# Two attentions of a one-core layer chain: another order of the steps, other PSUM banks, and turns by identity products

## The reference, cut to what matters

```python
def global_latent_attn(x, ...):            # local: k, v straight from x, and a window of 32
    q = split_heads(x @ wq, 16)
    latent = x @ w_kv_down                 # 32 wide
    k, v = split_heads(latent @ w_k_up, 4), split_heads(latent @ w_v_up, 4)
    q, k = qk_norm(rope(q)), qk_norm(rope(k))
    return merge_heads(sdpa(q, repeat_kv(k), repeat_kv(v), causal)) @ wo
x = x + global_latent_attn(rmsnorm(x, norm1_w), ...)
x = x + local_gqa_attn(rmsnorm(x, norm2_w), ...)
```

```python
xn = layernorm(x) * ln_g + ln_b
q, k, v = (xn @ W + b for each of q, k, v)      # 16 heads of width 8
w = softmax(q . k * scale, over the keys)
y = (w . v).reshape(B, T, 128)
```

## Time and profile before

| what | before |
|---|---|
| median of three runs | 2624.93 us (2624.47 to 2628.53) |
| the profiled execution, and its span | 2637.31 us, 2635.2 us |
| mean granted TensorE clock, share of full speed | 0.843 |
| PE busy | 2160.3 us (82%), 13860 matmuls |
| PE weight loads busy | 1691.5 us (64%) |
| DVE busy | 1468.8 us (56%) |
| ACT busy | 1000.2 us (38%) |

### The profile page before, as it was taken

How to read it: one execution, slowest core, us unless ns; L and a number is a source line. 1 busy time by engine, 2 the same in 40 slices (tenths; PEclk the granted TensorE clock), 3 DMA queues, 4 the chain that set the end, 5 groups by cost and what they waited for, 6 DMA issues and landing times. The chain is left out here.

```text
span 2635.2 us, 40558 instructions
## 1 busy us (share of the span) xinstructions
PE 2160.3 (82%) x13860; PEld 1691.5 (64%) x13860; DVE 1468.8 (56%) x3930; ACT 1000.2 (38%) x2247; POOL 131.4 (5%) x191
## 2 busy tenths in 40 slices
PE   3588777766997788499899989999979997588875
PEld 2344444435996322399899967888879995355543
DVE  6633334365666899756632226777742227655547
ACT  2244333333222332122244435555534444333434
POOL 2100000020000100100000000000000000000000
PEclk9776756677998899599989989999979998666678
DMA  5000000000000000000000004444300000000000
GB/s 155 2 1 0 0 1 0 0 28 1 1 0 1 0 0 0 32 1 0 1 1 0 0 19 132 125 125 124 123 12 0 0 0 0 1 1 0 0 1 16
DMA packets 47119, 59.65 MB, mean 23 GB/s; under 512 B 7089, under 2 KB 44689, under 8 KB 46323
## 3 DMA queue, kind: packets, MB, share of 16 engines
q1 hardware_dynamic: 47023, 58.43, 7.3%
HBM read 32.20 MB, written 26.21 MB: 22 GB/s over the span
## 5 line engine op out<-in xcount | busy, mean ns | idle before, releaser
L701 ACT ACTIVATE m2a_hid<-psum,m_b 128x256 f32<-128x256 f32 x256 | 100.2, 474 | 114.6 <-PE psum L55 114.5
L701 ACT ACTIVATE m2b_hid<-psum,m_b 128x256 f32<-128x256 f32 x256 | 100.2, 474 | 114.6 <-PE psum L55 114.5
L686 PE MATMUL psum<-m_w,m2a_hid 128*128 128x128 f32 x1024 | 126.2, 277 | 0.0
L686 PE MATMUL psum<-m_w,m2b_hid 128*128 128x128 f32 x1024 | 126.2, 277 | 0.0
L686 PEld LDWEIGHTS psum<-m_w,m2b_hid 128*128 128x128 f32 x1024 | 122.1, 194 | 0.6
L686 PEld LDWEIGHTS psum<-m_w,m2a_hid 128*128 128x128 f32 x1024 | 122.1, 194 | 0.6
L719 DVE SCALAR_TENSOR_TENSOR m2b_acc<-psum,m2b_gates,m2b_acc 128x128 f32<-128x128 f32 x128 | 39.0, 347 | 148.7 <-PE psum L686 148.7
L719 DVE SCALAR_TENSOR_TENSOR m2a_acc<-psum,m2a_gates,m2a_acc 128x128 f32<-128x128 f32 x128 | 39.0, 347 | 148.3 <-PE psum L686 148.3
L2026 ACT ACTIVATE a_p<-a_p,a_nmax 128x256 f32<-128x256 f32 x128 | 64.0, 500 | 143.3 <-DVE a_nmax L2053 143.3
L1769 DVE TENSOR_REDUCE a_nmax<-psum 128x2 f32<-128x512 f32 x128 | 83.0, 687 | 50.3 <-PE psum L1610 50.3
L1056 DVE TENSOR_TENSOR_SCAN a1s_clamped<-a1s_clamp_coef,a1s_bounds 128x1024 f32<-128x1024 f32 x48 | 108.6, 2265 | 0.0
(11 more groups left out here) (608 smaller groups left out, 5728.7 us busy)
## 6 DMA issues: line engine op xcount, KB each, us to landing
a_scratch<-a_pos SPq DMA_DIRECT2D x64, 384.0 KB, 2.7
a_shifted<-a_scratch SPq DMA_DIRECT2D x64, 256.0 KB, 3.1
m_w<-in_m_w SPq DMA_DIRECT2D x1, 2048.0 KB
arena<-in_m_w SPq DMA_DIRECT2D x1, 2048.0 KB, 9.2
arena<-in_m_up SPq DMA_DIRECT2D x1, 1760.0 KB, 7.1
a_w<-in_a_w SPq DMA_DIRECT2D x1, 1536.0 KB, 7.8
out<-X SPq DMA_DIRECT2D x1, 1024.0 KB, 5.1
m_down<-in_m_down SPq DMA_DIRECT2D x1, 880.0 KB
```

The source lines that it names most:

```text
L686: last = nc.tensor.matmul(ps_y(e % 2)[:, t * D:(t + 1) * D], hid[:, e % 2, c * SEQ + t * P:c * SEQ + (t + 1) * P], m.m2_w2[:, e, c, :], st ...
L701: last = nc.scalar.activation(hid[:, e % 2, c * SEQ:(c + 1) * SEQ], ps_up(e % 2)[:, c * SEQ:(c + 1) * SEQ], ACT.Gelu, bias=m.m2_b1[:, e * ...
```

## The change

In both functions the list of steps at each g is another, and some steps write to other banks.

- Grouped attention, PE: turn_back, `end_a`, `end_b` and `start_a` to `start_d` stand at other groups; `ps_y` lies in bank 4 instead of 7; start_d waits for normalise (n, 0) and for end_c of the unit before the present one (y_used). The ten transposes of start_d become ten products with `ident_r`, a float32r copy of the identity, the stack being the stationary operand as before.
- Grouped attention, DVE, ACT and GpSimd: steps regrouped accordingly; the input's norm is computed two units ahead instead of one, for which `threaded_two_ahead` unrolls six copies of the unit instead of four.
- a3: turn_back goes to bank 7 (j = 0, 1) or 5 (j = 2, 3), one group later, as does ACT's move_values; `values` waits for move_values (av_moved) instead of normalise; start_b stands behind values; turn_stack, turn_shifted and turn_back have new waits for their banks; the 24 transposes of a unit become products with `ident_r`.

The diff; its last pieces, from ps_back as a function on, are of a3.

```diff
+def threaded_two_ahead(eng, first, unit, tail):
+
+    first()
+    unit(0, 0, False, True, True)
+    with eng.Fori(0, NB // 2 - 2) as i:
+        unit(1, 2 * i + 1, True, True, True)
+        unit(0, 2 * i + 2, True, True, True)
+    unit(1, NB - 3, True, True, True)
+    unit(0, NB - 2, True, True, False)
+    unit(1, NB - 1, True, False, False)
+    tail(1, NB - 1)
...
-        ps_y = m.psum[:, 7, SEQ:2 * SEQ]
+        ps_y = m.psum[:, 4, 0:SEQ]
...
             def start_d(u, n):
                 pe.wait_ge(qk_ready, n + 1)
                 if not isinstance(n, int) or n:
-                    pe.wait_ge(o_ready, 4 * n - 2)
+                    pe.wait_ge(o_ready, 4 * n - 3)
+                if not isinstance(n, int) or n > 1:
+                    pe.wait_ge(y_used, n - 1)
                 for t in range(PAIR):
                     for j in range(4):
-                        nc.tensor.transpose(m.psum[:, 4 + j // 2, (j % 2) * SEQ + t * P:(j % 2) * SEQ + (t + 1) * P],
-                                            qs[:, t, KV * j:KV * (j + 1), :].rearrange("p h f -> p (h f)").bitcast(F32), m.ident[:, :])
-                    last = nc.tensor.transpose(ps_back[:, t * P:(t + 1) * P], ks[:, t, :, :].rearrange("p h f -> p (h f)").bitcast(F32), m.ident[:, :])
+                        nc.tensor.matmul(m.psum[:, 4 + j // 2, (j % 2) * SEQ + t * P:(j % 2) * SEQ + (t + 1) * P],
+                                         qs[:, t, KV * j:KV * (j + 1), :].rearrange("p h f -> p (h f)"), ident_r[:, :], start=True, stop=True)
+                    last = nc.tensor.matmul(ps_back[:, t * P:(t + 1) * P], ks[:, t, :, :].rearrange("p h f -> p (h f)"), ident_r[:, :], start=True, stop=True)
                 last.then_inc(qkT_ready, 1)
 
...
 
             def turn_back(u, n, j):
                 pe.wait_ge(av_moved, 4 * n + j + 1)
-                if j:
+                if j or not isinstance(n, int) or n:
                     pe.wait_ge(o_ready, 4 * n + j)
-                elif not isinstance(n, int) or n:
-                    pe.wait_ge(y_used, n)
+                if j == 1 and (not isinstance(n, int) or n < NB - 1):
+                    pe.wait_ge(kT_ready, n + 2)
                 for t in range(PAIR):
                     last = nc.tensor.transpose(ps_back[:, t * P:(t + 1) * P], ov[:, j % 2, t * P:(t + 1) * P], m.ident[:, :])
                 last.then_inc(back_ready, 1)
...
-                    if next and g == 6:
-                        start_d(1 - u, n + 1)
+                    if g == 0 and prev:
+                        turn_back(1 - u, n - 1, 2)
+                        values(1 - u, n - 1, 3)
+                    if g == 2 and prev:
+                        turn_back(1 - u, n - 1, 3)
+                    if g in (4, 6):
+                        turn_back(u, n, g // 2 - 2)
                     if g in (2, 4, 6):
                         values(u, n, g // 2 - 1)
-                    if g == 0 and prev:
-                        values(1 - u, n - 1, 3)
-                    if next and g == GROUPS - 1:
+                    if g < 3 and next:
+                        (start_a, start_b, start_c)[g](1 - u, n + 1)
+                    if g == 3 and prev:
+                        end_a(1 - u, n - 1)
+                    if g == 4 and prev:
+                        end_b(1 - u, n - 1)
+                    if g == 5 and next:
+                        start_d(1 - u, n + 1)
+                    if g == 7 and next:
                         pe.wait_ge(e_ready, GROUPS * n + g)
                         ready(n + 1)
                         scores(1 - u, n + 1, 0)
-                    if g in (4, 5, 7):
-                        turn_back(u, n, {4: 0, 5: 1, 7: 2}[g])
-                    if prev and g == 1:
-                        turn_back(1 - u, n - 1, 3)
-                    if prev and g == 2:
-                        end_a(1 - u, n - 1)
-                    if prev and g == 3:
-                        end_b(1 - u, n - 1)
-                    if next and g in (1, 2, 3):
-                        {1: start_a, 2: start_b, 3: start_c}[g](1 - u, n + 1)
...
+                start_a(1, 1)
+                start_b(1, 1)
                 start_e(0, 0)
...
-                    if next and g == 1:
-                        start_b(1 - u, n + 1)
-                    if prev and g == 1:
-                        normalise(1 - u, n - 1, 3)
-                    if next and g == 0:
-                        start_a(1 - u, n + 1)
-                    if prev and g == 3:
-                        end_c(1 - u, n - 1)
-                    if prev and g == 5 and local:
-                        residual_end(nc, dve, m, xn, n - 1)
-                    if next and g == 4:
+                    if g in (0, 2) and prev:
+                        normalise(1 - u, n - 1, 2 + g // 2)
+                    if g == 3 and next:
                         start_d(1 - u, n + 1)
+                    if g == 4 and next:
+                        start_d2(1 - u, n + 1)
                     if g == 4:
                         normalise(u, n, 0)
-                    if next and g == 5:
-                        start_d2(1 - u, n + 1)
-                    if g == 5:
+                    if g == 5 and prev:
+                        end_c(1 - u, n - 1)
+                    if g == 5 and next:
+                        start_e(1 - u, n + 1)
+                    if g == 6 and prev and local:
+                        residual_end(nc, dve, m, xn, n - 1)
+                    if g == 6 and later:
+                        start_a(u, n + 2)
+                    if g == 6:
                         normalise(u, n, 1)
-                    if next and g == 7:
-                        start_e(1 - u, n + 1)
-                    if g == 7:
-                        normalise(u, n, 2)
+                    if g == 7 and later:
+                        start_b(u, n + 2)
...
-        ps_av, ps_back = m.psum[:, 6, 0:SEQ], m.psum[:, 6, SEQ:2 * SEQ]
+        ps_av = m.psum[:, 6, 0:SEQ]
+        ps_back = lambda j: m.psum[:, 7 if j < 2 else 5, 0:SEQ]
...
-                        last = nc.tensor.transpose(out[:, j, t * P:(t + 1) * P], st[:, t, a, heads, :].rearrange("p h f -> p (h f)").bitcast(F32),
-                                                   m.ident[:, :])
+                        last = nc.tensor.matmul(out[:, j, t * P:(t + 1) * P], st[:, t, a, heads, :].rearrange("p h f -> p (h f)"), ident_r[:, :],
+                                                start=True, stop=True)
...
+                    if r == 1 and (not isinstance(n, int) or n > 1):
+                        pe.wait_ge(o_ready, 4 * n - 4)
...
             def turn_shifted(u, n, half):
                 pe.wait_ge(shift_ready, 2 * n + half + 1)
+                if half == 0 and (not isinstance(n, int) or n):
+                    pe.wait_ge(o_ready, 4 * n - 2)
                 turn_heads(ps_x, 0, half).then_inc(shift_turned, 1)
...
             def values(u, n, j):
                 pe.wait_ge(e_ready, GROUPS * n + 2 * j + 2)
                 if j or not isinstance(n, int) or n:
-                    pe.wait_ge(o_ready, 4 * n + j)
+                    pe.wait_ge(av_moved, 4 * n + j)
...
             def turn_back(u, n, j):
                 pe.wait_ge(av_moved, 4 * n + j + 1)
-                for t in range(PAIR):
-                    last = nc.tensor.transpose(ps_back[:, t * P:(t + 1) * P], ov[:, j % 2, t * P:(t + 1) * P], m.ident[:, :])
+                if j in (1, 3):
+                    pe.wait_ge(o_ready, 4 * n + j)
+                elif j == 0 and (not isinstance(n, int) or n < NB - 1):
+                    pe.wait_ge(moved, 4 * n + 7)
+                elif j == 2 and (not isinstance(n, int) or n < NB - 1):
+                    pe.wait_ge(nmax_ready, HEADS * n + 2 * HEADS)
+                for t in range(PAIR):
+                    last = nc.tensor.transpose(ps_back(j)[:, t * P:(t + 1) * P], ov[:, j % 2, t * P:(t + 1) * P], m.ident[:, :])
...
                     if g == 0 and prev:
+                        turn_back(1 - u, n - 1, 2)
                         values(1 - u, n - 1, 3)
-                    if g == 1 and prev:
+                    if g == 2 and prev:
                         turn_back(1 - u, n - 1, 3)
+                    if g in (4, 6):
+                        turn_back(u, n, g // 2 - 2)
+                    if g in (2, 4, 6):
+                        values(u, n, g // 2 - 1)
                     if g == 1 and next:
                         start_a(1 - u, n + 1)
                     if g == 2 and next:
                         start_b(1 - u, n + 1)
-                    if g in (2, 4, 6):
-                        values(u, n, g // 2 - 1)
                     if g == 7 and next:
                         turn_shifted(1 - u, n + 1, 0)
-                    if g in (3, 5, 7):
-                        turn_back(u, n, g // 2 - 1)
                     if g == 3 and next:
                         turn_stack(1 - u, n + 1)
```

(65 more changed lines are left out.)

18 lines of the change are left out of this document (12 added, 6 removed).

## The result

The changed kernel takes 2619.32 us (median of 20 runs) beside 2630.56 us for the kernel before in the same rounds: ratio 0.9945, 95% interval 0.993 to 0.9961. It is faster, by 11 us at the medians and some 14 by the ratio; either is less than half of the 36 that the sum gave, and 2619 lies above the forecast's range (2552 to 2612).

The account below looks back on a forecast made before the run. PE was taken to bound the three stages. Waits removed, new waits, a3 and start-up (-27.2 + 12.5 - 40.9 + 6.1 + 10.6 + 2.5) sum to -36.4 us, scaled to 2589 us at the median; range 2552 to 2612.

Parts of the forecast that it names:

- The grouped waits: Grouped attention, PE: three waits (turn_back, first scores, stacks' turn) all go, -27.2 us global and -40.9 us local.
- The new wait: Grouped attention, PE: start_d waits for end_c to have read bank 4, +12.5 us global and +6.1 us local.
- a3's waits: a3, PE: values' wait goes (-12.1 us), turn_stack gains 10.3 and turn_shifted 12.4; together +10.6 us.
- Start-up: Grouped stages: DVE's norm of unit 1 and identity copy ahead of start_e delay kT, +2.5 us for both.
- The turns: Three stages, PE: 352 turns as float32r identity products still wait for their loads; price changes by 0, bounds -32 to +32 us.
- Rival C: The granted clock falls in the three stages and the kernel is slower, 2654 us if a third falls; chance 0.08.
- B: Rival on PE's turns: a turn takes its product's columns alone, -68 us in all, 2557 us; chance 0.13.
- D: Rival on PE's turns: product and load do not overlap, turns dearer, -4 us in all, 2620 us; chance 0.07.

Follow-up runs that it names:

- e1: The changed kernel with all 352 turns as transposes again instead of identity products: 2567.03 us, ratio 0.9754 to the kernel before.
- f3: The changed kernel with each identity product moving the identity twice, 256 columns, except the last turn of each bank: 2601.95 us, ratio 0.9883 to the kernel before.
- g3: The changed kernel with each turn a plain float32 product with the float32 identity, in two instructions: 2605.47 us, ratio 0.9895 to the kernel before.
- g5: The changed kernel with 256-column float32r identity products, and the last turn of each bank as a transpose: 2556.60 us, ratio 0.9722 to the kernel before.

## Why the prediction was wrong

- **The grouped waits: right.** All counted as gone are gone, but for the 1.5 us above. The new wait was put at 12.5 and 6.1 us and measured 17.8 (16.3 of it ended by end_c) and 11.3; inside its bounds (5.6 to 22, 0 to 20), its cause as named.
- **a3's waits: right in sum, not in parts.** turn_stack +12.0 (10.3 forecast), turn_shifted +8.5 (12.4), a small one that I had not named, 2.3. The waits for exponentials that went, 5.2 in all, were not in the sum either.
- **Start-up: 0, not 2.5.** The first exponentials come at 138.1 us in both, and from the last global to the first local ones it is 26.3 us before and 25.6 after.
- **The turns: this step failed.** "So a product of half the columns still waits for its load, and the turns' price changes by 0." The spacing is as said; but I priced a turn by its spacing and kept each stage's share of full clock from the earlier trace rows. The turns lowered the granted clock of their stages (local 0.62 to 0.67 beside 0.72 to 0.90 with transposes, a3 0.58 beside 0.65), and that price is 52 us (e1 beside the changed kernel). As f3, g3 and g5 bear out, it comes where a product's columns are through before its load; the gap in PE itself was worked out, not seen. Rival C named that mechanism, with a chance of 0.08, and its sign came true in a3, a clock below 0.60; its time, 2654, did not, for the order's gain was larger than it reckoned. It had "nine tenths of the columns stay as they are" set against it; the other tenth was enough.
- **The order: its gain was mis-sized the other way.** Without the products it is worth 63 us (2567.03 beside 2630.56; 69 beside the runs of before on the same chip), not 36. PE also got more of the clock in the new order: global 0.70 before, 0.76 to 0.83 in the five kernels with transposes; local 0.65 before, 0.72 to 0.90. That it did because the waits went is my reading. The forecast of 36 lost 52 through the products and gained 27 that it had not counted, which leaves 11. So it is in part luck that the changed grouped stages came out near the sum (-13.9 and -30.7): in the same order with transposes, e1 shows -22 and -62.
- B and D are out: the turns' spacing did not change (0.21 us at half clock, as the earlier trace rows). The Trainium skill ("Perfetto Trace Analysis", section "Transposes") asks for transposes here, and e1 agrees, 52 us, though by the clock and not by the price of a turn.

## What to carry to other kernels

A step that costs the same from start to start can still cost time if it leaves the engine idle inside: where the granted clock has two levels, price a change by what PE does in that time, and treat the clock's share in a stage as an unknown with a price of its own. One profile of each kernel does not fix that share: the medians of several executions are what the kernels are compared by. A product in a shorter operand type, with a load that takes as long as before, bought nothing here, and it lost more than half of what a better order had won. Test the two halves of such a change apart before keeping both.

## What was not expected of the hardware

A float32 identity product in two instructions, twice the turns' time, did not make the kernel slower than the float32r one (2605 us over two executions, beside 2619). And the stages' clock is not a fixed share: kernels with the same code of the local stage ran it in 124 to 140 us. What sets where it settles is left open, as is the price of a float32r turn in other surroundings.
